# Attention probabilities turned for all four heads by VectorE blocks and SBUF to SBUF transfers of head pairs

## The reference, cut to what matters

```python
q = _rmsnorm(einsum(x, Wq), q_norm_w)            # 32 heads of 128
k = _rmsnorm(einsum(x, Wk), k_norm_w)            # 8 heads, each for 4 query heads
v = einsum(x, Wv)
q, k = _rope(q, pos), _rope(k, pos)
k_all = concatenate([k_cache[block_table], k])   # 512 cached keys and 128 new ones
v_all = concatenate([v_cache[block_table], v])
scores = where(valid, einsum('bqhd,bkhd->bhqk', q, k_all) * SCALE, -1e30)
o = einsum('bhqk,bkhd->bqhd', softmax(scores), v_all)
return einsum('bse,de->bsd', o, Wo)
```

## Time and profile before

| | us |
|---|---|
| median of three runs | 1301.07 (1300.37 to 1304.16) |
| span of the profiled execution | 1299.0 |
| PE busy | 1249.3 (96%) |
| DVE busy | 985.6 (76%) |
| ACT busy | 837.8 (64%) |
| POOL busy | 836.1 (64%) |

### The profile page before, as it was taken

One profiled execution on the slowest core, in us unless ns is written; L12 is line 12 of the kernel. 1 busy time (PEld: TensorE's weight loads), 2 busy tenths in 40 slices (PEclk: granted clock), 3 DMA queues, 4 the chain that ended last, 5 costly groups with the idle time before them and its releaser, 6 DMA issues. The chain is left out here.

```text
span 1299.0 us, 26260 instructions
## 1 busy us (share of the span) xinstructions
PE 1249.3 (96%) x7496; PEld 1074.6 (83%) x7496; DVE 985.6 (76%) x2388; ACT 837.8 (64%) x2505; POOL 836.1 (64%) x787
## 2 busy tenths in 40 slices
PE   5799997799999999999999999999999999999988
PEld 4677775688888888888888888888888888888878
DVE  3567857467888878887888778878888888788766
ACT  2667777466767676666766776676666767666731
POOL 1656656475767676758665876687667766775741
PEclk9899998899999999999999999999999999999999
DMA  7546554345455555555555555555555455455441
GB/s 264 204 170 243 206 217 151 104 115 146 133 139 134 140 140 142 143 139 134 146 136 146 137 144 131 139 137 144 134 143 140 131 143 143 126 138 141 134 133 65
DMA packets 288945, 191.48 MB, mean 147 GB/s; under 512 B 151201, under 2 KB 256674, under 8 KB 287778
## 3 DMA queue, kind: packets, MB, share of 16 engines
q1 hardware_dynamic: 287792, 189.64, 51.2%
q10 hardware_dynamic: 1010, 0.17, 0.1%
HBM read 143.60 MB, written 79.69 MB: 172 GB/s over the span
## 5 line engine op out<-in xcount | busy, mean ns | idle before, releaser
L1779 POOL TENSOR_TENSOR b_p_l<-b_moved,b_p_h 128x640 fp32r<-128x640 f32 x128 | 200.9, 1570 | 163.9 <-PE ps L1375 93.8
L1514 ACT ACTIVATE b_pf<-b_sm,b_mn 128x640 f32<-128x640 f32 x256 | 212.4, 830 | 127.5 <-DVE b_mn L1624 127.5
L1624 DVE CUSTOM_DVE_ANT_0 b_sm<-ps,mask_row,b_rstd 128x640 f32<-128x640 f32 x256 | 225.0, 879 | 53.7 <-PE ps L1301 48.8
L1526 ACT ACTIVATE b_p_h<-b_moved 128x640 fp32r<-128x640 f32 x128 | 94.7, 740 | 160.0 <-DMA b_moved<-blocks_of_probs 158.8
L1660 DVE SCALAR_TENSOR_TENSOR b_hacc<-ps,b_ri,b_hacc 128x512 f32<-128x512 f32 x248 | 182.4, 736 | 4.6 <-PE ps L1301 4.3
L1299 PE MATMUL ps<-b_w_h,x1t_h 128*128 128x512 f32 (+1 forms) x512 | 178.8, 349 | 0.1
L1299 PE MATMUL ps<-b_kt_h,b_qt_h 128*128 128x320 f32 x512 | 169.5, 331 | 4.6 <-DVE b_mn L1624 4.2
L1300 PE MATMUL ps<-b_w_l,x1t_h 128*128 128x512 f32 (+1 forms) x512 | 173.4, 339 | 0.0
L1301 PE MATMUL ps<-b_w_h,x1t_l 128*128 128x512 f32 (+1 forms) x512 | 173.2, 338 | 0.0
L1301 PE MATMUL ps<-b_kt_h,b_qt_l 128*128 128x320 f32 x512 | 159.3, 311 | 0.0
L1300 PE MATMUL ps<-b_kt_l,b_qt_h 128*128 128x320 f32 x512 | 159.2, 311 | 0.0
(11 more groups left out here) (177 smaller groups left out, 3371.1 us busy)
## 6 DMA issues: line engine op xcount, KB each, us to landing
blocks_of_probs<-b_blk SPq DMA_DIRECT2D x128, 320.0 KB, 2.4
b_moved<-blocks_of_probs SPq DMA_DIRECT2D x512, 80.0 KB, 2.1
kv_of_batch<-in_kv SPq DMA_DIRECT2D x128, 256.0 KB
b_ck<-kv_of_batch SPq DMA_DIRECT2D x64, 256.0 KB, 4.0
b_cv<-kv_of_batch SPq DMA_DIRECT2D x256, 64.0 KB, 1.9
raw<-in_w SPq DMA_DIRECT2D x32, 384.0 KB, 3.2
raw<-in_wo SPq DMA_DIRECT2D x32, 256.0 KB, 2.8
a_xt<-in_xt SPq DMA_DIRECT2D x8, 256.0 KB, 6.7
```

The costliest lines, as they stand in the source:

```text
L1514: act.activation(pf[:, h % 2], sm[:, h % 2], ACT.Exp, bias=mn[:, m.b % 2, h:h + 1], scale=-1.0, accum_out=rs[:, m.b % 2, h:h + 1]).then_in ...
L1526: act.activation(blocks_of(p_h[:, :, h * P:(h + 1) * P]), moved[:, d].rearrange("p (a t j) -> p a t j", a=LT, j=QUAD), ACT.Copy).then_inc( ...
L1624: dve.tensor_tensor_reduce(sm[:, h % 2], score_row, mask_row[:, m.b], rstd[:, m.b % 4, h:h + 1], -MASKED, ALU.add, ALU.min, mn[:, m.b % 2, ...
L1779: pool.tensor_tensor(blocks_of(p_l[:, :, h * P:(h + 1) * P]), moved[:, d].rearrange("p (a t j) -> p a t j", a=LT, j=QUAD), blocks_of(p_h[: ...
```

## The change

- All four heads go the way of blocks. `turn_probs`, `high` and `low` of the heads that PE turned are gone, with `turned_row` and its two banks. DVE calls `turn_blocks` four times a slot.
- Two heads, a pair, are moved together, from SBUF to SBUF, without DRAM between: `blocks_across` issues four transfers of 160 KB for a pair, each from 32 partitions of `blk` to all 128 of `moved`. The key order inside a tile of 128 changes with it (partition 4 s + q), and `value_rows` and `new_keys` follow it.
- ACT copies a pair at once (`high(m, pair)`, 128x1280), POOL writes its low part (`low_probs(m, pair)`). Pair 0 is done in the slot, pair 1 in the next.
- The exponential is written in place, into `sm`; `pf` is gone. `minima` waits for `turn_blocks` of two heads before.
- Scores have two regions, banks 0 and 1 for even heads, 2 and 3 for odd ones, so `scores` waits for `minima` of two heads before.
- The sum of the key's rope products moves from POOL to DVE (`key_sum`), its scaling to ACT (`turned_key`). `rope_keys` is gone.
- On DVE `minima(m, 3)` comes before `queries(one)`. On SP the weight chunks come before the second pair's transfers and `value_rows`.
- `squares_out` becomes bf16, and small tiles of the last stage are merged. The upper value products stand ahead of the fourth head's scores, as before.

```diff
-        SC, PT, OT, SM, PJQ, PJK = 0, 2, 4, 5, 6, 7
+        SC, OT, SM, PJQ, PJK = (0, 2), 4, 5, 6, 7
...
-                    sp.dma_start(cv[q * PSIZE:(q + 1) * PSIZE], rows_of).then_inc(cv_in, 16)
+                    sp.dma_start(cv[q::LT], rows_of).then_inc(cv_in, 16)
...
+            def blocks_across(m, pair):
+
+                sp.wait_ge(blk_sb, REP * m.n + 2 * (pair + 1))
+                wait(sp, ml_sb, 2 * (m.n - 1) + pair + 1)
+                for a in range(LT):
+                    place = moved[:, pair].rearrange("p (h a n) -> p h a n", h=2, a=LT)[:, :, a]
+                    sp.dma_start(place, blk[pair][a * QUAD:(a + 1) * QUAD, :]).then_inc(moved_in[pair], 16)
 
             def slot(m, one, two, last):
-                if m:
-                    blocks_away(m, 0)
-                    blocks_back(m, 0)
-                    blocks_away(m, 1)
+                blocks_across(m, 0)
                 if two:
                     key_rows(two)
-                blocks_back(m, 1)
-                if two:
-                    value_rows(two)
                 if m.b in (2, 3, 4, 5):
                     chunk(m.g + 1, m.b - 2)
...
+                blocks_across(m, 1)
+                if two:
+                    value_rows(two)
...
# PE
-                wait(pe, mn_sb, REP * m.n + h)
+                wait(pe, mn_sb, REP * m.n + h - 1)
...
-                turn_probs(m, 2)
                 if two:
                     project_q(two)
...
-                turn_probs(m, 3)
...
# ACT
+            def turned_key(m):
+                act.wait_ge(kab2_sb, m.n + 1)
+                act.wait_ge(rstd_sb, m.n + 1)
+                act.activation(ka[:], kb[:], ACT.Copy, scale=rstd[:, m.b % 4, REP:REP + 1]).then_inc(kr_sb, 1)
...
-                act.activation(pf[:, h % 2], sm[:, h % 2], ACT.Exp, bias=mn[:, m.b % 2, h:h + 1],
+                act.activation(sm[:, h % 2], sm[:, h % 2], ACT.Exp, bias=mn[:, m.b % 2, h:h + 1],
...
+            def high(m, pair):
+                act.wait_ge(moved_in[pair], 16 * LT * (m.n + 1))
                 wait(act, pvh_ps, m.n)
+                act.activation(pair_of(p_h, pair), moved_pair(pair), ACT.Copy).then_inc(mh_sb, 1)
...
                 if last:
-                    high(last, 3)
+                    high(last, 1)
                 exponent(m, 1)
...
-                high_moved(m, 0)
+                if one:
+                    turned_key(one)
                 if last:
                     output(last)
                 exponent(m, 3)
-                high(m, 2)
+                high(m, 0)
                 if one:
                     new_keys(one)
                     cache_values(one)
-                high_moved(m, 1)
...
# DVE
+            def key_sum(m):
+                dve.wait_ge(kab_sb, m.n + 1)
+                dve.tensor_tensor(kb[:], ka[:], kb[:], ALU.add).then_inc(kab2_sb, 1)
...
+                wait(dve, moved_in[h // 2], 16 * LT * m.n)
+                dve.transpose(head_in_pair(h), by_tile(sm[:, h % 2])).then_inc(blk_sb, 1)
...
                 if one:
                     new_values(one)
-                if last:
-                    low(last, 3)
+                    key_sum(one)
                 minima(m, 2)
                 turn_blocks(m, 1)
                 if before:
                     accumulate(before, 3)
...
+                minima(m, 3)
                 if one:
                     queries(one)
-                minima(m, 3)
+                turn_blocks(m, 2)
                 if last:
                     output(last)
                     invert(last)
-                low(m, 2)
+                turn_blocks(m, 3)
                 if one:
                     new_keys(one)
...
# POOL
+            def low_probs(m, pair):
+                pool.wait_ge(mh_sb, 2 * m.n + pair + 1)
                 wait(pool, pv_ps, m.n)
+                pool.tensor_tensor(pair_of(p_l, pair), moved_pair(pair), pair_of(p_h, pair), ALU.subtract).then_inc(ml_sb, 1)
...
                 if one:
                     rms(one)
-                    rope_keys(one)
+                if last:
+                    low_probs(last, 1)
...
-                low_moved(m, 0)
+                low_probs(m, 0)
                 if one:
                     cache_values(one)
-                low_moved(m, 1)
                 if two:
                     rope_queries(two)
```

More of the change, by code:

```diff
@@ L932, in phase3 @@
     ht_h, ht_l = (x1t_l[:, 4], x1t_l[:, 5]), (x1t_l[:, 6], x1t_l[:, 7])
-    b_gate = sb("b_gate", [P, NR])
-    first = sb("first", [P, NR])
+    b_gate, first = small_rows[:, 0:NR], small_rows[:, NR:2 * NR]
+    sc, weight = [small_rows[:, 8 * (1 + i):8 * (2 + i)].rearrange("p (k r) -> p k r", k=2) for i in range(2)]
+    top, expert = small_rows[:, 24:26], small_rows[:, 26:28]
     most = sb("most", [P, 2, MAXR])
[L936 to L940, removed]
     lowt = sb("lowt", [P, 2, P], F32R)
@@ L948, in phase3 @@
     bth_sb, btl_sb = sem("bth_sb"), sem("btl_sb")
-    small = ((b_gate, "b_gate"), (first, "first"), (most, "most"))
+    small = ((b_gate, "b_gate"), (first, "first"), (most[:], "most"))
     def flat(ap):
@@ L1170, in phase2 @@
         mn_sb, exp_sb, ri_sb = sem("mn_sb"), sem("exp_sb"), sem("ri_sb")
-        ph_sb, pl_sb = sem("ph_sb"), sem("pl_sb")
-        blk_sb, blk_out, moved_in = sem("blk_sb"), [sem(f"blk_out{h}") for h in BY_DMA], [sem(f"moved_in{h}") for h in BY_DMA]
+        blk_sb, moved_in = sem("blk_sb"), [sem(f"moved_in{pair}") for pair in range(2)]
         mh_sb, ml_sb = sem("mh_sb"), sem("ml_sb")
@@ L1579, in slot @@
                     exponent(one, 0)
-            scalar_first(act, (q_weights, kv_weights, squares, new_kv, queries, cache_keys, new_keys, cache_values))
+            scalar_first(act, (q_weights, kv_weights, squares, new_kv, queries, turned_key, cache_keys, new_keys, cache_values))
             slots(act, slot)
-            high(end, 3)
+            high(end, 1)
             h_out(act, 2)
@@ L1710, in low_kv_weights @@
                 dve.tensor_tensor(w_l[:, :, cols], raw[:, :, cols], w_h[:, :, cols], ALU.subtract).then_inc(wkvl_sb, 1)
-            vector_first(dve, (rope_products, new_values, queries, new_keys, minima, low_weights, low_kv_weights))
+            vector_first(dve, (rope_products, new_values, key_sum, queries, new_keys, minima, low_weights, low_kv_weights))
             slots(dve, slot)
             accumulate(end.before(), 2)
-            low(end, 3)
             accumulate(end.before(), 3)
@@ L1808, in _ @@
             pool.wait_ge(const_sb, 1)
-            gpsimd_first(pool, (q_weights, kv_weights, rope_queries, rms, rope_keys, cache_keys, cache_values))
+            gpsimd_first(pool, (q_weights, kv_weights, rope_queries, rms, cache_keys, cache_values))
             slots(pool, slot)
+            low_probs(end, 1)
             pool_ffn(pool)
```

132 lines of the change are left out of this document (39 added, 93 removed).

## The result

The changed kernel takes 1407.56 us in the median of five runs (1403.24 to 1435.26), beside 1301.07 for the kernel before: 1.081 times as long, 95% interval 1.078 to 1.084. The forecast was 1303 with a range up to 1330.

The account below looks back on a forecast made before the run. TensorE was taken as saturated. Transposes gone -65, query split +38, GpSimd's late packs +30.5, score regions -1.5 gave +2 on the 1299.0 span, so 1303 us with 2.1 for the median; range 1280 to 1330.

Parts of the forecast that it names:

- Ten transposes off TensorE: Transposes of heads 2 and 3 leave TensorE: 1.02 us a slot, 65 us over 64 slots.
- the query split as a new stall: queries(one) behind minima(m, 3) on VectorE delays TensorE's query projection: 0.61 us in 62 slots, 38 us given back.
- plain slot: One group and batch without special weight work: 15.66 us before, 14.64 without new stalls, 15.25 with the late query projection.
- the ring: Loop from turn_blocks(m, 1) through transfer, copy, keys and VectorE to the next such turn: 10.8 us plus the transfer time.
- GpSimd's packs: Low parts as two 2.97 us packs, hidden in plain slots, late around weight splits: 4.0 us a group, 30.5 in all.
- The wait for b_ra: TensorE's query transposes wait in b = 7 after GpSimd's late b = 6 work: 1.58 us a group.
- key_sum, priced at 0.44 between 0.2 and 0.5: The key's sum added on VectorE ahead of minima(m, 2), priced at 0.44 us with its own wait.
- the sum: Whole kernel: -65 + 38 + 30.5 - 1.5 = +2 us on the 1299.0 span, so 1303 with 2.1 for the median.
- The transfer, L = 4.0 from 3.3 to 5.0: L, from a pair's first transfer issue to ScalarE's copy: 1.8 latency + 4 x 0.55 = 4.0 us.
- the transfer sets the pace: Rival: 32-partition reads at half rate make the transfer 5.0 us, the slot 15.8, the time 1327; chance 0.20.
- the Door 1 rule: For the pair's transfers: 32 neighbouring partitions reach only 8 of 16 DMA ports, which would halve the read rate.
- The prediction's own slope: GpSimd's losses in each group change by about 2.5 times the transfer time's change: 8 us down, 9 up.

Follow-up runs that it names:

- ks_same128: ks_psum with each transfer from all 128 partitions to the same 128, in 256 runs of 640 bytes, output not the reference's; 1318.28 us (one run).
- ks_psum: The changed kernel with the key's cosine product written to PSUM in all items but the first, so key_sum reads one operand there; 1359.32 us (1.047 of before).
- same128_q: ks_same128 with queries(one) ahead of minima(m, 3) on VectorE, output not the reference's; 1304.44 us (one run).
- head_cv1: ks_psum with each head moved behind its own block turn, queries(one) ahead of minima(m, 3), four value transfers made one; 1316.39 us (1.011).

## Why the prediction was wrong

The steps, in its own order:

- *Ten transposes off TensorE* and *the query split as a new stall*: right in kind. The wait stands at the projection, released by b_qt_l, 48 times: 41.2 us in the changed kernel, 22.3 where nothing else is late. The plain slot of ks_same128 is 15.29, foretold 15.25. Without the stall it is 14.78, 0.51 less and not 0.61, because the ring then stands at 14.8. Over the kernel it is 14 us instead of 38: only the slots b = 2, 3, 4 and 7 gain, and the others, with the late packs and around them, last as long with the split in either place (b=6 17.9 and 17.9, the slot before it 15.35 and 15.35).
- *GpSimd's packs*: 2968 ns for 2.97, high 1275 for 1.26, and 17 waits of the lows for p_l of up to 2.2 us, for two a group of 1.8. The wait for b_ra comes 8 times in ks_same128, 10.0 us: in each b=7 but the last group's, 1.24 us instead of 1.58, and once at the start. turned_key takes 0.39 on ScalarE, priced 0.2 to 0.3; no run shows what that costs.
- *key_sum, priced at 0.44 between 0.2 and 0.5*: **the first step that failed.** It was bounded by the distance of 128x128 products, which read one operand from PSUM, while key_sum reads both from SBUF. It took 1.46 in the mean and up to 3.1, and stands at the head of the ring, ahead of minima(m, 2). Cost: 48 us. A row of the trace of before could have warned: VectorE's c_weight, 128x4, both tensor operands in SBUF, beside GpSimd:

```profile
1256.69 1.10 DVE L1075 SCALAR_TENSOR_TENSOR c_weight<-c_sc,c_top,c_first 128x4 f32<-128x4 f32 x1
```

```profile
1256.48 1.29 POOL L1113 TENSOR_TENSOR x1t_l<-raw,x1t_l 128x512 fp32r<-128x512 f32 x1 [3.16 <-ACT x1t_l L1054]
```

  1.10 us for four columns, and the end falls 0.02 behind GpSimd's, which was running when it started. The Trainium skill, "SBUF — State Buffer", Who interferes with whom, says that a VectorE instruction with two SBUF inputs waits for a GpSimd instruction that reads SBUF, and the other way round, because they share a port. The runs agree with the first half; that GpSimd waits for VectorE no row here shows. It was not weighed; the largest doubt of the sum was looked for in the transfer alone.
- *The transfer, L = 4.0 from 3.3 to 5.0*: **the second that failed.** It measured 5.6 in the median, beyond the upper bound. Two terms were too small: the issues, 0.62 to 0.73 apart instead of 0.435, and the rate out of 32 partitions, which had been taken from loads into them and from stores of 128. The rival "the transfer sets the pace" was right in mechanism, and the Door 1 rule that stood behind it as well; 0.20 was too little for it, and its L of 5.0 too short. Cost of the 32 source partitions: 41 us, by ks_same128, which still has L at 4.55.
- *The ring, 10.8 + L, deciding from 4.45*: right in kind, and 0.5 too long. It measured 10.27 + L in all ten profiles named above. In parts: 0.87 before the first issue, 1.18 from the copy to new_keys on ScalarE (priced 1.26), 0.29, and 7.93 instead of 8.38 on VectorE, from new_keys to the next turn_blocks(m, 1), in ks_psum as in same128_q. Of these 0.45, 0.15 is key_sum, which takes 0.29 where it is free, and the rest steps that follow one another more closely: from turn_blocks(m, 0) to the next minimum 0.76 instead of 0.96. So the ring decides from L = 4.98, not 4.45: at the rival's own L of 5.0 it would have cost next to nothing, and its 1327 came of a ring too long and an L too short.
- *The sum*: with key_sum free and L at 4.5 the measured time is 1318.3. The prediction's own slope, 2.5 times the change of L in each group, gives 1303 + 8 x 2.5 x 0.5 = 1313. The groups of that kernel, from one first issue of b=0 to the next, last 126.7 to 130.6 us, beside the 126.0 walked out. Most of the 5 us left is the clock, a term that the sum put at nothing: it stands at 0.50 in three stretches, each in a slot b=1, one of them here:

```profile
532.00:535.00 3.00, 3.00 (x9) 2.31 (x8) 1.62 (x3) 2.45 (x4) 2.58 (x3) 0.50 0.61 105
```

  These three slots last 17.6, 18.0 and 17.7 us, where four without it last 16.45 to 16.49 (walked out 16.47): 3.9 us together.
- *The range*: it ended at the ring with L = 5.0. Both failures lie on one chain, minima(m, 2), turn_blocks(m, 1), transfer, so they add.

What stays open: why a transfer from SBUF takes 0.62 us and more to issue, and the four value loads 0.63 as well, when the same queue took 0.435 in the earlier trace rows. In head_cv1 the same key load was issued in 0.36 behind an idle queue and in 0.61 behind eight transfers, so it goes with what is in flight and not with the kind of transfer alone; no run here separates the two. What else in the transfer makes L 4.55 with all 128 partitions is open as well, and so is head_cv1 with the weight chunk behind the second pair.

## What to carry to other kernels

Before a small elementwise step is moved from GpSimd to VectorE, look where its operands lie: with both in SBUF it cost here what was left of the instruction running on GpSimd, up to 3.1 us for 0.29. One operand in PSUM avoided it. A transfer out of 32 neighbouring partitions should be priced from such a transfer; if the trace has none, the range must reach to half the rate and past it (half the rate gave 5.0 us here, 5.6 were measured), and the steps around it must be walked as a ring, with the queue's own issues as a second ring. Engine time taken off TensorE is worth only the distance to the next wait, here 0.4 us of 1.02 a slot before anything went wrong. And new stalls of TensorE can be paid twice, once as the wait and once at the lower clock behind it.

## What the runs showed of the hardware

- A VectorE instruction of 0.29 us with both operands in SBUF lasted up to 3.1 us while a GpSimd instruction ran, and 0.29 with one operand in PSUM, with nothing else changed.
- Transfers of 160 KB, four in a row, landed in 3.3 us out of 32 partitions each and in 2.3 out of 128 (medians); the order of the four quarters alone changed the kernel by 18 us.
- 640-byte pieces instead of 5120-byte ones cost 20 us over 512 transfers; spreading them over 128 target partitions cost nothing.
- Issues on SP's queue followed one another by about 0.65 us when it was full, and 22 of them made it the bound of a kernel with 15.4 us a slot.
- Behind stalls (0.33 and 1.22 us in the case shown) TensorE's granted clock fell from 1.00 to 0.50 for a stretch, in which products of 512 columns were 0.43 us apart instead of 0.23: 19 times in the changed kernel's second stage, never in that of the kernel before behind its first 30 us.
